# Attention and mixture-of-experts layer on one core: 32 expert pairs in two alternating scatter chains, four tables loaded together at the end, last block reordered

## The chip, the cores and the metric

The kernel runs on one core of one Trainium2 chip. The metric is the device time of one execution in microseconds (us); lower is better. The times shown are medians of several executions, and a profile is one further execution.

## The reference

The input x has 4 sequences of 1024 tokens with 256 values each. Two sublayers follow one another, each with a layer norm ahead and a layer norm behind it, and a residual sum.

```python
x = x + _layernorm(attn(_layernorm(x)))   # 16 heads, 4 key/value heads, head size 128, causal, rope
x = x + _layernorm(ffn(_layernorm(x)))    # 64 experts, 6 for each token, plus a shared expert
# ffn, per token t:   y[t] = sum over its experts e of w[t,e] * down_e(silu(x @ gate_e) * (x @ up_e))
#                     out[t] = y[t] + down_s(silu(x @ gate_s) * (x @ up_s))
# routing: top 4 of 8 groups, then the 6 best of 64 experts; at most 48 tokens for an expert
```

## The kernel before

Three blocks of instructions follow one another, and no engine enters the next block before all engines have left the last. The function attention fills the span up to about 1781 us. It is not changed. The function last_quad follows (to about 1847 us), and then the function experts (to the end).

**last_quad** finishes what is left of the last 512 tokens: the norms of y and x1, the logits, the choice of experts, and the lists of tokens of every expert (VectorE's largest, rounds of MAX8 and MATCH_REPLACE8). Beside that the shared expert runs over eight parts of 512 tokens: gate_up and down on TensorE, gate_tanh and shared_out on ScalarE, shared(n) on VectorE, which consists of two instructions (lines 1535 and 1540). shared_out(n) sends its part to the first of four tables in HBM, named sums, by a DMA that ScalarE issues (line 1444). ScalarE's last instructions in this block wait for all these DMAs (y_out, line 1487). Near the end GpSimd stores the routing weights (line 1495), waits for all seven of its stores and for seven counts of index_done, and issues six gathers of token rows (line 1514, LEAD = 6). Its memset of the gather buffer (line 1498) stands ahead of the first inverse root, for whose result VectorE waits before it applies x1 (line 1555). SyncE loads the weights of 40 experts into w_early.

**experts** works through 32 pairs of experts. For pair j TensorE transposes the gathered rows (line 1863), multiplies by gate and up (1875), transposes the hidden values (1883) and multiplies by down (1890). ScalarE and VectorE copy and scale the halves of the result (1829, 1768) into a ring of four y buffers. GpSimd then adds the 128 rows to the tables in HBM by an indirect DMA with an add (line 1729). The rows of one expert never meet twice, but rows of different pairs may, so a scatter waits until the one before it in its chain has landed. There are two chains with two tables each:

```python
def in_second(j):
    return j % 2 == 1 and j < 2 * TURNS      # TURNS = 14
```

So the second chain holds 14 pairs, the last one pair 27, and pairs 28 to 31 all go to the first chain, one after another. A buffer of y is filled again when the scatter four pairs back has landed. Ahead of each scatter GpSimd issues the gather of the pair LEAD ahead, once VectorE and TensorE have let go of the buffer (ring of 8).

SyncE loads the last 24 experts (line 1694), then x1 (1696), and, when the second chain has ended, its two tables m2 and m3 into the space of used weights (1702), unit by unit. A unit is 4 tiles of 128 tokens; there are 8. VectorE adds m3 to m2 (joined, line 1779) in between the last steps of the pair loop, two units in each of the last four steps. When the first chain has ended, SyncE loads m0 and m1, each unit after its join (1709).

The last stage works unit by unit: GpSimd adds m2 to m0 (1742), TensorE adds m0 and m1 in PSUM by an identity matrix (1912), VectorE takes the statistics (1793, 1796) and the reciprocal (1801), ScalarE the root (1845) and the scaling (1853), GpSimd the shift (1737, 1738), VectorE adds the residual (1785), SyncE stores (1713). The small tiles of this stage are rings of two, and residual(u-1) stands between the statistics and the reciprocal of unit u.

## Time and profile before

| what | value |
|---|---|
| median of 3 executions | 2049.85 us (2048.86 to 2051.9) |
| the profiled execution's own time | 2050.17 us |
| its span, first to last instruction | 2048.4 us |
| mean granted TensorE clock | 0.956 of full speed |
| busy share of the span: TensorE matmul, VectorE, ScalarE, GpSimd | 93%, 65%, 56%, 63% |
| last_quad | 1781 to 1847 us |
| pair loop, first matmul to last scatter landed | 1847 to 1990 us |
| last stage | 1990 to 2048 us |

The span is what the rows below are measured in; 1.77 us of the profiled execution's time lie around it. The busy shares are averages over very different stages: TensorE's 93% come from attention, and in the last 200 us it is often idle. Times in the rows are microseconds from the start of the span.

### The profile page before, as it was taken

The numbers are of one execution on the slowest core, as the hardware profiler recorded it, in microseconds if no ns is written. First come the engines' busy times: TensorE is split into PE (matmuls) and PEld (weight loads), VectorE is DVE, ScalarE is ACT, GpSimd is POOL, SyncE is SP. The second block draws the span as 40 slices with busy tenths as digits, with TensorE's granted clock in tenths as the row PEclk, the third lists the DMA queues.
The fourth block names the chain that finished last, engine by engine and source line by source line (L and its number), as shares of the span: only waits on it lengthen the run. The fifth ranks groups of instructions, "written<-read, shape, count | busy, mean of one in ns | idle before, by whom it ended". The sixth has DMA issues, their size and how long they took to land. (4 is left out here: it accounts for less than half of the span.)

```text
span 2048.4 us, 34361 instructions
## 1 busy us (share of the span) xinstructions
PE 1895.5 (93%) x11846; PEld 1566.2 (76%) x11846; DVE 1330.8 (65%) x3149; ACT 1154.0 (56%) x2632; POOL 1284.4 (63%) x1061
## 2 busy tenths in 40 slices
PE   5999999999999999999999999999999999787926
PEld 4888888888888888888888888888888888543412
DVE  5566666667767677777667667676676778762324
ACT  3556666666656665566565665666655655333413
POOL 5758576666666765758485766676666755214733
PEclk8999999999999999999999999999999999995658
DMA  5005000001110100000100100001101000298476
GB/s 178 16 27 164 29 21 6 22 6 31 48 52 6 42 1 22 11 27 32 58 21 6 42 6 27 6 21 57 32 6 42 1 17 17 105 357 284 67 220 210
DMA packets 77292, 120.22 MB, mean 59 GB/s; under 512 B 9639, under 2 KB 57717, under 8 KB 75873
## 3 DMA queue, kind: packets, MB, share of 16 engines
q1 hardware_dynamic: 65264, 92.61, 13.6%
q0 software_dynamic: 7248, 12.72, 2.6%
q10 hardware_dynamic: 4608, 12.68, 1.9%
q8 instruction: 98, 1.61, 0.3%
q14 instruction: 74, 0.60, 0.1%
HBM read 90.34 MB, written 38.53 MB: 63 GB/s over the span
## 5 line engine op out<-in xcount | busy, mean ns | idle before, releaser
L561 PE MATMUL s_ps<-kT,q 128*128 128x512 f32 (+3 forms) x2304 | 584.3, 371 | 13.9 <-POOL q L1136 7.9
L824 DVE TENSOR_TENSOR pT<-t_ps,pT 128x512 fp32r<-128x512 f32 (+3 forms) x768 | 401.0, 550 | 191.0 <-ACT pT L969 189.8
L811 DVE TENSOR_REDUCE neg_max<-s_ps 128x1 f32<-128x640 f32 (+7 forms) x512 | 384.6, 751 | 110.8 <-PE s_ps L561 103.9
L561 PEld LDWEIGHTS s_ps<-kT,q 128*128 128x128 f32 x2304 | 408.3, 192 | 61.6 <-ACT probs L958 11.6
L586 PE MATMUL av_ps<-pT,v 128*128 128x512 f32 x1728 | 442.2, 400 | 2.7 <-DVE pT L824 2.7
L1121 POOL TENSOR_TENSOR k_roped<-raw,sinT 64x512 f32<-64x512 f32 x316 | 406.7, 1287 | 24.3
L969 ACT ACTIVATE pT<-t_ps 128x512 fp32r<-128x512 f32 (+3 forms) x768 | 348.7, 490 | 129.8 <-PE t_ps L571 125.0
L958 ACT ACTIVATE probs<-s_ps,neg_max 128x640 f32<-128x640 f32 (+7 forms) x512 | 381.9, 746 | 63.3 <-DVE neg_max L811 61.0
L586 PEld LDWEIGHTS av_ps<-pT,v 128*128 128x128 f32 x1728 | 311.8, 189 | 67.1 <-DVE pT L824 7.8
L571 PE MATMUL t_ps<-k_ident,probs 128*128 128x128 f32 x2304 | 340.1, 274 | 11.6 <-DVE pT L824 7.9
L1118 POOL TENSOR_TENSOR k_roped<-raw,cosT 128x512 f32<-128x512 f32 x158 | 204.4, 1294 | 220.1 <-ACT raw L930 201.3
L571 PEld LDWEIGHTS t_ps<-k_ident,probs 128*128 128x128 f32 x2304 | 263.2, 140 | 37.4 <-ACT probs L958 12.8
L598 PE MATMUL misc_ps<-w_o,avT 128*128 128x256 f32 x1536 | 237.9, 291 | 15.5 <-DVE y L856 8.1
L598 PEld LDWEIGHTS misc_ps<-w_o,avT 128*128 128x128 f32 x1536 | 204.9, 189 | 33.5 <-ACT raw L930 12.9
L856 DVE SCALAR_TENSOR_TENSOR y<-misc_ps,inv_sum,y 128x256 f32<-128x256 f32 x448 | 214.9, 480 | 14.1 <-PE misc_ps L598 6.1
L1123 POOL TENSOR_TENSOR raw<-k_roped 128x512 f32<-128x512 f32 x158 | 202.8, 1283 | 12.4
L518 PE MATMUL misc_ps<-xT,w_q 128*128 128x256 f32 x1524 | 204.2, 283 | 1.7 <-DVE y L856 1.7
L518 PEld LDWEIGHTS misc_ps<-xT,w_q 128*128 128x128 f32 x1524 | 194.6, 190 | 3.7 <-DVE y L856 2.3
L829 DVE TENSOR_TENSOR avT<-av_ps,avT 128x512 fp32r<-128x512 f32 x128 | 88.6, 692 | 136.5 <-ACT avT L976 136.3
L976 ACT ACTIVATE avT<-av_ps 128x512 fp32r<-128x512 f32 x128 | 76.3, 596 | 162.2 <-PE av_ps L586 159.5
L939 ACT ACTIVATE q<-raw 128x512 fp32r<-128x512 f32 x128 | 80.6, 630 | 150.7 <-POOL raw L1123 150.7
L1136 POOL TENSOR_TENSOR q<-raw,q 128x512 fp32r<-128x512 f32 x128 | 163.1, 1288 | 1.8 <-ACT q L939 1.8
(245 smaller groups left out, 1877.4 us busy)
## 6 DMA issues: line engine op xcount, KB each, us to landing
w_early<-in_expert_w SPq DMA_DIRECT2D x5, 2560.0 KB, 26.6
w_early<-sums SPq DMA_DIRECT2D x24, 512.0 KB, 8.8
k_staged<-in_wpack SPq DMA_DIRECT2D x47, 256.0 KB, 2.9
sums<-sums ACTq DMA_DIRECT2D x2, 4144.0 KB, 22.9
k_staged<-in_wpack SPq DMA_DIRECT2D x16, 512.0 KB, 3.7
e_w_late<-in_expert_w SPq DMA_DIRECT2D x3, 2560.0 KB
k_xw<-in_x SPq DMA_DIRECT2D x4, 1024.0 KB, 5.8
k_xb<-in_x SPq DMA_DIRECT2D x4, 1024.0 KB, 5.9
```

The costliest lines, as they stand in the source:

```text
L518: last = pe.matmul(bank("q", macro, half)[:, h * 256:(h + 1) * 256], w_q[:, s, half, c, h * HD:(h + 1) * HD], pair(xT[:, b % 2, a, c], m), ...
L561: last = pe.matmul(out, q[:, macro % 2, a, h, int(big)], kT[:, g % 2, s, lo:hi], start=(n == 0), stop=(n == 2))
L571: last = pe.transpose(t_ps[n % 2][:, j * P:(j + 1) * P], probs[:, r % 3, (first + j) * P:(first + j + 1) * P], ident[:])
L586: last = pe.matmul(av_ps[:], v[:, g % 2, a, j], pT[:, s, part_slot(p) + j], start=(j == 0 and n == 0), stop=(j == blocks - 1 and n == 2))
L598: last = pe.matmul(misc_ps[:, h * HID:(h + 1) * HID], avT[:, a, 2 * half + h], w_o[:, s, 2 * half + h], start=(n == 0), stop=(n == 2))
L811: dve.reduce_max(neg_max[:, r % 16:r % 16 + 1], s_ps[:, r % 2, 0:(row_tile(r) + 1) * P], AX.X, negate=True).then_inc(max_ready, 1)
L824: dve.tensor_tensor(lo, t_ps[n % 2][:, 0:count * P].rearrange("p (j n) -> p j n", n=P), hi.bitcast(F32), ALU.subtract).then_inc(t_lo, 1)
L856: last = dve.scalar_tensor_tensor(target[:, t], src, inv, y[:, t], ALU.mult, ALU.add)
L958: act.activation(probs[:, r % 3, 0:width], s_ps[:, r % 2, 0:width], ACT.Exp, bias=neg_max[:, r % 16:r % 16 + 1], accum_out=row_sum[:, r % ...
L969: act.activation(pT[:, 0, slot + first:slot + first + count, r % 4], t_ps[n % 2][:, 0:count * P].rearrange("p (j n) -> p j n", n=P), ACT.C ...
L1118: pool.tensor_tensor(shape(cosed), shape(raw[:, n % 2]), table(cosT, 0, P), ALU.mult).then_inc(cos_done, 1)
L1121: pool.tensor_tensor(shape(rope[64 - lo:128 - lo]), shape(raw[lo:hi, n % 2]), table(sinT, lo, hi), ALU.mult).then_inc(sin_done, 1)
```

## The change

In last_quad: TensorE's down(0) goes ahead of transpose_x2, ScalarE's gate_tanh(1) ahead of x1_apply. VectorE's shared(0) is split, its first half goes ahead of the x1 step, and shared(1) goes from the third round of largest to the place after shared_up(0). GpSimd's memset goes behind the row stores. The four instructions that make the routing weights go from the end of VectorE's work to the place ahead of the second set of rounds. LEAD becomes 8, so eight gathers are issued. ScalarE's wait for y_out leaves the block; SyncE takes it as its first instruction in experts, and GpSimd ahead of its first scatter.

In experts: TURNS becomes 16, so the chains alternate to the end with 16 pairs each. The early load and the joins inside the pair loop are gone. After the pair loop SyncE loads all four tables unit by unit; VectorE adds m3 to m1 while GpSimd adds m2 to m0, TensorE sums the two, and the last unit is summed by VectorE alone. LAG = 2 makes the small tiles rings of three, and the residual of a unit comes after the join of the unit three behind it.

```diff
-TURNS = 14
+TURNS = 16
+LAG = 2
-    RING, LEAD = 8, 6
+    RING, LEAD = 8, 8
...
             gate_up(1)
+            down(0)
             transpose_x2()
-            down(0)
...
             gate_tanh(0)
+            gate_tanh(1)
             x1_apply()
-            gate_tanh(1)
...
-            for i in range(2):
-                act.wait_ge(y_out[i], 32 * B)
...
-            link(pool.memset(index.gathered[:], 0.0))
...
+            link(pool.memset(index.gathered[:], 0.0))
             pool.wait_ge(weight_done, 1)
             store_weights(LAST)
             pool.wait_ge(stored, 7 * 16)
-            pool.wait_ge(index_done, 7)
+            pool.wait_ge(index_done, 5)
...
             stats(xw, kept.y_mv)
             dve.memset(last_rows[:], 0.0)
+            shared_gate(0)
             dve.wait_ge(rstd_done, 1)
...
-            shared(0)
+            shared_up(0)
+            shared(1)
...
-                if i == 2:
-                    shared(1)
...
             shared(3)
+            (product, sum, reciprocal and scale of the routing weights)
             dve.wait_ge(key_in, 1)
...
-            (the same four instructions)
...
         def _(sp):
+            for i in range(2):
+                sp.wait_ge(y_out[i], 32 * B)
...
-            sp.wait_ge(y_ready, last_pair(2))
-            sp.wait_ge(added[1], 16 * TURNS)
-            for u in range(UNITS):
-                for dst, table in ((m2, 2 * TABLE), (m3, 3 * TABLE)):
-                    sp.dma_start(unit(dst, u), ...).then_inc(loaded[u], 16)
             sp.wait_ge(y_ready, PAIRS)
             sp.wait_ge(added[0], 16 * (PAIRS - TURNS))
             for u in range(UNITS):
-                sp.wait_ge(joined, u + 1)
-                for dst, table in ((m0, 0), (m1, TABLE)):
+                for n, dst in enumerate((m0, m1, m2, m3)):
+                    if u == 0 and n == 2:
+                        sp.wait_ge(added[1], 16 * TURNS)
                     sp.dma_start(unit(dst, u), ...).then_inc(loaded[u], 16)
...
+                if j == 0:
+                    for i in range(2):
+                        pool.wait_ge(y_out[i], 32 * B)
...
-                for u in range(max(first, 0), first + 2):
-                    dve.wait_ge(loaded[u], 32)
-                    dve.tensor_tensor(unit(m2, u), unit(m2, u), unit(m3, u), ALU.add).then_inc(joined, 1)
...
+            def join(u):
+                dve.wait_ge(loaded[u], 64)
+                if u < UNITS - 1:
+                    dve.tensor_tensor(unit(m1, u), unit(m1, u), unit(m3, u), ALU.add).then_inc(joined, 1)
+                else:
+                    dve.tensor_tensor(unit(m1, u), unit(m1, u), unit(m3, u), ALU.add)
+                    link(dve.tensor_tensor(unit(m0, u), unit(m0, u), unit(m2, u), ALU.add))
+                    link(dve.tensor_tensor(unit(m0, u), unit(m0, u), unit(m1, u), ALU.add))
...
+            for u in range(UNITS):
+                join(u)
+                if u:
+                    stats_of(u - 1)
+                if u > LAG:
+                    residual(u - LAG - 1)
+            stats_of(UNITS - 1)
+            for u in range(UNITS - LAG - 1, UNITS):
+                residual(u)
...
             for u in range(UNITS):
                 root_of(u)
+                if u:
+                    scale_of(u - 1)
+            scale_of(UNITS - 1)
...
-            for u in range(UNITS):
+            for u in range(UNITS - 1):
                 pe.wait_ge(padded, u + 1)
+                pe.wait_ge(joined, u + 1)
```

## Rows read from the trace of the kernel before

**Rows 1.** Timeline of SyncE's queue, 1840 to 1995: start, issue time, line, tensors, count.

```profile
1847.22 5.93 SPq L1694 DMA_DIRECT2D e_w_late<-in_expert_w  x3
...
1957.01 20.55 SPq L1702 DMA_DIRECT2D w_early<-sums  x16
1990.16 0.36 SPq L1709 DMA_DIRECT2D e_w_late<-sums  x1
```

**Rows 2.** Timeline of VectorE, first join: start, duration; in brackets idle time before it.

```profile
1963.34 1.23 DVE L1779 TENSOR_TENSOR w_early<-w_early 128x1024 f32<-128x1024 f32 x1 [8.13 <-DMA w_early<-sums]
```

**Rows 3.** Chain of work that ended last: start, length, what.

```profile
1856.33 8.20 DMA sums<-k_xb,i_to_row
...
1881.51 10.02 DMA i_gathered<-rows,i_from_row
...
1953.30 3.64 DMA sums<-k_xb,i_to_row
...
1969.43 8.11 DMA sums<-k_xb,i_to_row
...
2024.83 3.71 PE e_gu_ps L1912 x8
```

**Rows 4.** Timeline of GpSimd in last_quad.

```profile
1783.09 2.25 POOL L1498 MEMSET i_gathered<- 128x2560 f32 x1
...
1829.64 1.41 POOL L1495 DMA_DIRECT2D rows<-k_row_w  x2 [33.52 <-DVE k_row_w L1609]
1836.29 1.11 POOL L1514 DMA_INDIRECT i_gathered<-rows,i_from_row  x1 [5.24 <-DMA rows<-k_row_w]
```

**Rows 5.** Timeline of VectorE in last_quad.

```profile
1787.33 1.67 DVE L1555 SCALAR_TENSOR_TENSOR k_xb<-k_xw,k_y_rstd,k_xb 128x256 f32<-128x256 f32 x4 [4.15 <-POOL k_shift L248]
...
1793.04 0.73 DVE L1563 TENSOR_SCALAR k_xw<-k_xb,k_x_mv,k_x_rstd 128x256 f32<-128x256 f32 x2 [0.68 <-POOL k_x_shift L246]
...
1797.49 0.68 DVE L1535 SCALAR_TENSOR_TENSOR r_a<-r_th,r_gate 96x512 f32<-96x512 f32 x1
...
1827.79 0.42 DVE L1606 TENSOR_TENSOR k_spare<-k_score,k_picked 128x256 f32<-128x256 f32 x1
...
1829.25 0.18 DVE L1612 TENSOR_SCALAR i_from_row<-r_c 128x32 int32<-128x32 f32 x1
```

**Rows 6.** Timeline of ScalarE in last_quad: first tanh, last output issue.

```profile
1784.73 0.59 ACT L1434 ACTIVATE r_th<-r_gate 96x512 f32<-96x512 f32 x1 [5.10 <-PE r_gate L1356]
...
1840.51 0.98 ACTq L1444 DMA_DIRECT2D sums<-r_y  x2
```

**Rows 7.** Timeline of GpSimd, the scatters of pairs 8 and 28.

```profile
1891.19 1.60 POOL L1729 DMA_INDIRECT sums<-k_xb,i_to_row  x1 [1.89 <-DMA sums<-k_xb,i_to_row]
...
1956.28 1.55 POOL L1729 DMA_INDIRECT sums<-k_xb,i_to_row  x1 [1.43 <-issue]
```

**Rows 8.** Busy time by stretch: PE, PEld, DVE, ACT, POOL, clock, DMA share, GB/s.

```profile
1820.00:1830.00 10.00, 6.90 (x28) 4.02 (x27) 7.43 (x33) 2.28 (x4) 0.36 (x1) 0.94 1.04 403
...
1900.00:1910.00 10.00, 10.00 (x45) 4.14 (x43) 2.63 (x9) 3.76 (x12) 7.97 (x7) 0.50 0.40 66
...
2000.00:2005.00 5.00, 5.00 (x10) 2.21 (x9) 0.85 (x3) 0.00 (x0) 1.00 (x1) 0.72 1.10 348
```

**Rows 9.** Timeline of VectorE in the last stage.

```profile
2020.45 1.38 DVE L1785 TENSOR_TENSOR e_w_late<-e_w_late,w_early 128x1024 f32<-128x1024 f32 x1 [0.31 <-ACT e_w_late L1853]
...
2038.25 1.43 DVE L1793 BATCH_NORM_STATS2 e_stats<-e_y_ps 128x6 f32<-128x256 f32 x4 [0.99 <-PE e_y_ps L1912]
...
2043.84 1.23 DVE L1785 TENSOR_TENSOR e_w_late<-e_w_late,w_early 128x1024 f32<-128x1024 f32 x1 [2.55 <-ACT e_w_late L1853]
```

**Rows 10.** Timeline of GpSimd in the last stage, one unit's add.

```profile
2018.41 2.34 POOL L1742 TENSOR_TENSOR e_w_late<-e_w_late,w_early 128x1024 f32<-128x1024 f32 x1
```

**Rows 11.** Timeline of ScalarE, root and scaling of the last unit.

```profile
2040.12 0.30 ACT L1845 ACTIVATE e_root<-e_mv,e_eps 128x4 f32<-128x4 f32 x1 [0.35 <-DVE e_mv L1796]
2041.87 1.93 ACT L1853 ACTIVATE e_w_late<-e_y_ps,e_shift,e_rstd 128x256 f32<-128x256 f32 x4 [1.45 <-POOL e_shift L1738]
```

More of the change, by code:

```diff
@@ L1284, in __init__, with last_quad @@
         self.from_row, self.to_row = sb("from_row", [P, EXPERTS // 2], I32), sb("to_row", [P, EXPERTS // 2], I32)
-def last_quad(nc, consts, kept, index, rows, x1_rows, x2t_rows, y_rows, w_early, w_in, shared_in, gathered_in):
+def last_quad(nc, consts, kept, index, rows, x1_rows, x2t_rows, y_rows, w_early, w_in, shared_in, gathered_in, y_out):
     with ExitStack() as ctx:
@@ L1319, in last_quad @@
         gate_ready, up_ready, tanh_done, a_done, h_done = (sem(n) for n in ("gate_ready", "up_ready", "tanh_done", "a_done", "h_done"))
-        down_ready, y_read, y_out = sem("down_ready"), sem("y_read"), [sem(f"y_out{i}") for i in range(2)]
+        down_ready, y_read = sem("down_ready"), sem("y_read")
         block = ctx.enter_context(nc.Block())
@@ L1540, in shared @@
                 dve.scalar_tensor_tensor(h[:, n % 2], a[:, n % 2], 0.5, up_ps[n % 2][0:FF], ALU.mult, ALU.mult).then_inc(h_done, 1)
+            def shared(n):
+                shared_gate(n)
+                shared_up(n)
             def largest(at, left, i):
@@ L1619, in _, with experts @@
             shared(7)
-def experts(nc, consts, kept, rows, index, w_early, w_in, gathered_in, sums, x1_rows, out):
+def experts(nc, consts, kept, rows, index, w_early, w_in, gathered_in, sums, x1_rows, y_out, out):
     with ExitStack() as ctx:
@@ L1696, in _ @@
             sp.dma_start(x1.rearrange("p (b t) n -> p b t n", b=B), x1_rows.rearrange("b p t n -> p b t n")).then_inc(x1_in, 16)
-            sp.wait_ge(y_ready, last_pair(2))
-            sp.wait_ge(added[1], 16 * TURNS)
-            for u in range(UNITS):
-                first = u * UNIT * P
-                for dst, table in ((m2, 2 * TABLE), (m3, 3 * TABLE)):
-                    sp.dma_start(unit(dst, u), tiles(sums[table + first:table + first + UNIT * P])).then_inc(loaded[u], 16)
             sp.wait_ge(y_ready, PAIRS)
@@ L1706, in _ @@
                 first = u * UNIT * P
-                sp.wait_ge(joined, u + 1)
-                for dst, table in ((m0, 0), (m1, TABLE)):
-                    sp.dma_start(unit(dst, u), tiles(sums[table + first:table + first + UNIT * P])).then_inc(loaded[u], 16)
+                for n, dst in enumerate((m0, m1, m2, m3)):
+                    if u == 0 and n == 2:
+                        sp.wait_ge(added[1], 16 * TURNS)
+                    at = n * TABLE + first
+                    sp.dma_start(unit(dst, u), tiles(sums[at:at + UNIT * P])).then_inc(loaded[u], 16)
             for u in range(UNITS):
@@ L1842, in root_of, with scale_of @@
                 act.wait_ge(mv_ready, u + 1)
-                if u >= 2:
-                    act.wait_ge(rstd_ready, u - 1)
-                act.activation(root[:, u % 2], mv[:, u % 2, :, 1], ACT.Sqrt, bias=eps[:]).then_inc(root_done, 1)
+                if u > LAG:
+                    act.wait_ge(rstd_ready, u - LAG)
+                act.activation(ring(root, u), ring(mv, u)[:, :, 1], ACT.Sqrt, bias=eps[:]).then_inc(root_done, 1)
+            def scale_of(u):
+                act.wait_ge(shift_ready, u + 1)
+                for t in range(UNIT):
+                    last = act.activation(m0[:, u * UNIT + t], summed_tile(u, t), ACT.Identity, bias=ring(shift, u)[:, t:t + 1], scale=ring(rstd, u)[:, t:t + 1])
+                last.then_inc(normed, 1)
             act.wait_ge(act_done, 1)
@@ L1850, in _ @@
                 root_of(u)
-                act.wait_ge(shift_ready, u + 1)
-                for t in range(UNIT):
-                    last = act.activation(m0[:, u * UNIT + t], summed_tile(u, t), ACT.Identity, bias=shift[:, u % 2, t:t + 1], scale=rstd[:, u % 2, t:t + 1])
-                last.then_inc(normed, 1)
+                if u:
+                    scale_of(u - 1)
+            scale_of(UNITS - 1)
         @block.tensor
@@ L1902, in _ @@
                     down(s - 3)
-            for u in range(UNITS):
+            for u in range(UNITS - 1):
                 pe.wait_ge(padded, u + 1)
+                pe.wait_ge(joined, u + 1)
                 if u >= 4:
@@ L1929, in build @@
         gathered_in = [ctx.enter_context(nc.semaphore(f"gathered_in{i}")) for i in range(index.RING)]
-        last_quad(nc, args, kept, index, rows, x1_rows, x2t_rows, sums[0:TABLE], w_early, w_in, shared_in, gathered_in)
-        experts(nc, args, kept, rows, index, w_early, w_in, gathered_in, sums, x1_rows, out)
+        y_out = [ctx.enter_context(nc.semaphore(f"y_out{i}")) for i in range(2)]
+        last_quad(nc, args, kept, index, rows, x1_rows, x2t_rows, sums[0:TABLE], w_early, w_in, shared_in, gathered_in, y_out)
+        experts(nc, args, kept, rows, index, w_early, w_in, gathered_in, sums, x1_rows, y_out, out)
 def lay_out(inputs):
```

70 lines of the change are left out of this document (41 added, 29 removed).

## The prediction

> **What bounds the kernel now.** I read the chain of work that ended last first, because the busy shares say little about the last 270 us, where the whole change lies. From 1847 us on the chain is made of three things in turn: scatters and gathers whose landing somebody awaits, TensorE's matmuls, and then the summing stage [rows 3]. The timeline of SyncE's queue gives the three marks to keep: the last load of weights at 1847.22, the early load of two tables from 1957.01, and the first load of the other two at 1990.16 [rows 1]. From this last mark to the end of the span are 2048.4 - 1990.2 = 58.2 us.
>
> The reader should look at what happens between 1957 and 1990. The early load lies beside the last pairs. VectorE takes its queue in order, and its first join stands ahead of its work for pairs 30 and 31. It sat 8.13 us for the first unit's tables [rows 2] and then for the next. So the scatter of pair 29, due about 1960 (pair 28's at 1956.28 and a landing [rows 7]), went out at 1969.43, and under the load it took 8.11 us to land, where the one at 1953.30 took 3.64 [rows 3]. Three such scatters in one chain end at 1990. In the last stage the load of 8 units is not what holds: at 348 GB/s [rows 8] a unit of two tables, 1.05 MB, takes 3.01 us, and the whole stage takes 58.2.
>
> **The change part by part.**
>
> *Head, last_quad.* (a) Without the memset, 2.25 us [rows 4], the first inverse root ends that much sooner. VectorE applied x1 at 1787.33 [rows 5]. But the new shared_gate(0) stands ahead of it and needs the first tanh, which ends at 1784.73 + 0.59 = 1785.32 [rows 6], then takes 0.68 [rows 5]. So x1 starts at 1786.0: 1.3 us sooner. (b) shared(1), two instructions of 0.68, leaves the rounds of largest. It goes where VectorE sat 0.68 us for the second inverse root [rows 5], together with the half of shared(0) that moved forward: these two hide it. Gain 1.4, in all 2.7. Who is late now: nobody, since TensorE's down(0) ahead of the transposes falls into its own idle time before x2 is ready, and the logits come sooner, well ahead of VectorE. (c) The four instructions of the weights, 1829.25 - 1827.79 = 1.46 us [rows 5], now lie ahead of the rounds: the lists end at 1827.8 - 2.7 + 1.5 = 1826.6. TensorE turns them, which the weights used to hide, some 0.5 us, and the index is there about 1827.7. (d) GpSimd issued the first gather at 1836.29 because the weights' stores of 1829.64 had to land first [rows 4]. Those stores now go out well over 10 us sooner, because six rounds of largest and six smaller ones lie behind them, so the gathers start about 1828. Eight of them at 1.1 + 0.3 take 11 us and are issued by 1839.3. (e) The block ended with the landing of the shared outputs, at 1847.2 [rows 1], although ScalarE had issued the last at 1840.51 + 0.98 = 1841.5 [rows 6]. The wait is moved; the last issue is 1.2 sooner with the rest, 1840.3; I allow 1.0 for the meeting of the engines. experts starts at 1841.3, which is 5.9 us sooner. The moved waits: behind SyncE's stand the last weights and x1, which nobody needs for 40 us or more; behind GpSimd's stands the first scatter, whose rows are ready about when the outputs land, near 1846. If that cover were gone, the 5.9 would shrink to about 1. Bounds of the head: 1 to 7.
>
> *First pairs.* SyncE's bulk loads (12 MB: w_late and x1) start at the landing of y_out, so hardly sooner than before, and now run together. While they run a scatter takes 8.2 us [rows 3] and each chain holds one at a time, so pairs 0, 2, 4, 6, 8 follow one another at about 9 us, later less. With pair 0 at 1850.4 (1856.33 - 5.9) and loads that end about 1877, I get 1859.5, 1868.5, 1876.5 and pair 8 at 1883; before it was at 1891.19 [rows 7]. The 2.3 us beyond the head's 5.9 come from LEAD = 8: before, a gather of 10.02 us held TensorE [rows 3], and now it is issued two pairs sooner. The nearest bounds are 3 us (the bulk loads eat the head start) and 14.
>
> *Rest of the pair loop.* Before, pairs 8 to 28 took 1956.28 - 1891.19 = 65.1 us, 3.25 each [rows 7]: GpSimd's gather and scatter, or TensorE at half clock, 45 matmuls of 15 a pair in 10 us, 3.3 a pair [rows 8]. The new kernel has both, so I keep 65.1. Then three more, alternating, each after the landing of the one two back: (3.64 + 0.7) / 2 = 2.2 us each, 6.5. So pair 31 goes out at 1883 + 65.1 + 6.5 = 1954.6 and pair 30's landing starts the load at 1954.6 - 2.2 + 3.64 + 0.5 = 1956.5. Before, that mark was 1990.2. Of the 33.7 us between them 8.2 come from pair 8, and 25.5 from the last pairs: four scatters in one chain without stall or load would have ended about 1973 (1956.3 + 4 x 4.3), so 17 are the collision that is gone and 8 the alternation. Bounds: 1951, if TensorE has its full clock and GpSimd's eight pairs without a gather go at 2.2; 1967, if the half clock holds 3.5 us a pair to the end.
>
> *Load.* The price of the change: all 16 portions of 1.05 MB (two transfers each) now stand behind the pair loop. The first landed 1963.34 - 1957.01 = 6.3 us after its issue [rows 1, 2], the other 15 follow at 3.01: 51.5 us, and 1.1 us for the second portion, which waits for pair 31, in all 52.6. The rate is from a stretch without other work [rows 8]. The last unit is there at 1956.5 + 52.6 = 2009.1. Other work hides below it: a unit takes 6.0 us to load, GpSimd needs 2.34 [rows 10] and two small ones, TensorE 3.71 [rows 3], VectorE 1.23 for the join, 1.87 + 0.3 for statistics and root, 1.23 for the residual [rows 9, 11], so none is the bound. The stores come after the loads in SyncE's queue; six of 1.5 us fit below the tail.
>
> *Tail after the last unit.* VectorE sums it alone, 3 x 1.23 = 3.7. Then the statistics of unit 6 through its reciprocal, 2.4 with 0.2 for the reciprocal; residual 4, 1.23; statistics of unit 7 to the root's start, 2040.12 - 2038.25 = 1.9; root 0.3; ScalarE's scaling of units 6 and 7, because root 7 stands ahead of scale 6: 2 x 1.93; residual 1.23; then 2048.4 - 2045.07 = 3.3 for the store [rows 9, 11]. Sum 17.9.
>
> Before the tail stands one wait that the trace shows only at its edge. VectorE's residual at 2020.45 started while GpSimd's add of 2018.41 to 2020.75 ran, and took 1.38 instead of 1.23 [rows 9, 10]: an overlap of 0.3 cost 0.15. In the new stage GpSimd's add and VectorE's join start on the same semaphore in every unit. If one waits out the other, the join ends 2.34 + 1.23 after the landing, and VectorE's round of 4.8 us ends 7.2 after it. That is 1.2 more than the 6.0 of a unit, but it does not add up: the next join then asks 1.2 later and waits 1.2 less. The last unit has no such add, so the cost is 1.2 once. I take it, as if the wait were full, and keep 0 and 2.3 as its bounds; with the half that the row shows it would be 0.6. The Trainium skill ("SBUF — State Buffer", Who interferes with whom) says that VectorE with two SBUF inputs and GpSimd reading SBUF exclude each other for a whole instruction. By that rule the sum comes out as below, and by the half wait of the row 0.6 us sooner; at its edge the trace agrees in direction.
>
> **Sum.** 1956.5 + 52.6 + 1.2 + 17.9 = 2028.2 us of span; with 1.77 around it 2030.0, against 2050.17 of the profiled execution, 20.2 us less. The median of the runs is 0.3 below that execution, so 2029.7; I say 2030.
>
> **The rivals.**
>
> *TensorE keeps the half clock.* It ran at 0.50 through 1900 to 1910 though busy all the time [rows 8], so being busy doesn't bring it back at once. At that level, 1.2 GHz, the pair loop takes up to 3.5 us a pair and starts the load at 1967; in the sums a unit is 7.4 us (2 x 3.71) instead of 6.0, so unit 6 lags. For it: GpSimd's waits are gone, so TensorE is nearer to being the bound. Against: the clock was 0.72 and rising after 5 us of summing [rows 8]. With the pair loop alone at half clock the time is 2040.
>
> *All smooth.* Pair loop at full clock, bulk loads over sooner, load from 1951 or before: 2024.
>
> *The loads go faster than 348 GB/s.* The tables' own stretch does not, but from 1820 to 1830, with expert weights in larger rows, 403 GB/s were moved [rows 8]. At that pace 16.8 MB take 6.6 us less: 2023. The Trainium skill ("DMA: Bandwidth & Descriptors", Measured) has 425 GB/s for 16 MB in one piece; by that figure it would be 2021, an estimate from that page. The row of the same tensors speaks against it.
>
> *Slower: the load of four tables collapses.* The transfers now alternate among four regions of HBM. If a transfer took over 4.4 us instead of 3.01 (240 GB/s), 15 of them would eat the whole gain: that is the point from which it decides. At 220 GB/s it is 2056. For it: half of these bytes lay beside other work before and are now in the open, so every loss of rate counts twice. Against: two regions in turn already run at the full 348 [rows 8], and two more are the same kind of read.
>
> *It does not do what it says.* The head's gain and LEAD = 8 are taken back by bulk loads, and VectorE or the ring of y holds pairs 28 to 31 as before: 2050. The code leaves no wait of that kind.
>
> **How the numbers follow.** Forecast 0.60 (2030, its own range 2026 to 2035). Half clock 0.16 (2040), all smooth 0.11 (2024), faster loads 0.04 (2023), collapse 0.06 (2056), no gain 0.03 (2050). The range 2021 to 2041 leaves out the last two and the edges of the others, and it holds the bounds of the head (3 us less gained) and of the pair loop (5.5 us sooner to 10.5 later). Faster by over 0.2%, which is 4.1 us and about what a measurement of this kernel can tell from no change: 0.60 + 0.16 + 0.11 + 0.04 = 0.91; within it 0.03; slower 0.06.
>
> **What would show it.** First matmul of the block experts about 1841 and first gather about 1828 (before 1836.3). Scatter of pair 8 about 1883. No idle time of VectorE over 3 us between 1940 and 1955, and scatters of pairs 29 to 31 about 2.2 us apart. SyncE's first table load about 1956.5, 32 of them, units 6.0 us apart at 348 GB/s, the last landed about 2009. GpSimd's add and VectorE's join one after the other. 19 us from the last landing to the end. The prediction is wrong if the pair loop's bulk loads hold more than two scatters at 8 us each, if TensorE falls behind the loads, or if the rate is below 300 GB/s.

## The result, and the profile after

The median of the runs of the new kernel is 2030.77 us (2028.52 to 2033.01), that of the kernel before, run beside it, 2050.82: a ratio of 0.9906 with the interval 0.9893 to 0.9918. It is faster by 20.1 us, and the forecast was 2030. The profiled execution of after took 2028.52 us with a span of 2026.6, so 1.9 us lie around it. Attention ended later in it, and last_quad starts 1.07 us later than in the trace of before (1782.21 against 1781.14). All marks below are as the trace has them; where the shift matters I say so.

SyncE's queue (start and length in us, then line, operation and tiles) has the three marks that [rows 1] had:

```profile
1844.96 5.39 SPq L1711 DMA_DIRECT2D e_w_late<-in_expert_w  x3
...
1956.89 0.93 SPq L1722 DMA_DIRECT2D e_w_late<-sums  x2
1960.11 0.91 SPq L1722 DMA_DIRECT2D w_early<-sums  x2
```

The first table load goes out at 1956.89, as early as the old early load did, but now all 32 scatters lie before it. The two loads of 1960.11 are those of m2 and m3, which had to wait for pair 31. From there to the last load SyncE waits for nothing but its own queue.

GpSimd's timeline shows how the pair loop gets there (in brackets the idle time before, and what ended it):

```profile
1829.83 1.12 POOL L1512 DMA_INDIRECT i_gathered<-rows,i_from_row  x1 [14.67 <-DVE i_to_row L1622]
...
1854.31 1.63 POOL L1745 DMA_INDIRECT sums<-k_xb,i_to_row  x1 [0.30 <-issue]
...
1880.93 1.60 POOL L1745 DMA_INDIRECT sums<-k_xb,i_to_row  x1 [1.83 <-DMA sums<-k_xb,i_to_row]
...
1888.82 1.60 POOL L1745 DMA_INDIRECT sums<-k_xb,i_to_row  x1 [0.30 <-issue]
...
1937.54 1.60 POOL L1745 DMA_INDIRECT sums<-k_xb,i_to_row  x1 [0.30 <-issue]
...
1942.14 1.55 POOL L1745 DMA_INDIRECT sums<-k_xb,i_to_row  x1 [1.12 <-DMA sums<-k_xb,i_to_row]
...
1955.63 1.55 POOL L1745 DMA_INDIRECT sums<-k_xb,i_to_row  x1 [1.05 <-DMA sums<-k_xb,i_to_row]
1965.90 3.37 POOL L1759 TENSOR_TENSOR e_w_late<-e_w_late,w_early 128x1024 f32<-128x1024 f32 x1 [8.72 <-DMA w_early<-sums]
```

These are, in order, the first gather, then the scatters of pair 0, 6, 8, 23, 25 and 31, and the first add. Three stages can be told apart by what stands in the brackets. Up to pair 7 a landing releases half of the scatters (pairs 2, 5, 6 and 7), VectorE or TensorE most of the others. From pair 8 to pair 23 it is the issue itself: (1937.54 - 1888.82) / 15 = 3.25 us a pair, and GpSimd never waits. The last eight have no gather ahead of them, and go (1955.63 - 1937.54) / 8 = 2.26 us apart, and every odd pair goes out at the landing of the one two back, with an even pair close behind it. Pair 29 follows pair 28 after 2.46 us, where 13 us separated them in [rows 3, 7].

The chain of work that ended last, for the scatters in it and for the last load (start, length, what):

```profile
1857.61 7.47 DMA sums<-k_xb,i_to_row
...
1866.30 9.02 DMA sums<-k_xb,i_to_row
...
1946.59 3.65 DMA sums<-k_xb,i_to_row
...
1955.63 4.46 DMA sums<-k_xb,i_to_row
...
2000.36 8.67 DMA w_early<-sums
```

Beside the bulk loads a scatter takes 7.5 to 9.0 us to land, without them 3.65, as in [rows 3]. The last scatter, with two table loads beside it, takes 4.46. The last stage, on VectorE:

```profile
1978.37 3.01 DVE L1804 TENSOR_TENSOR e_w_late<-e_w_late,w_early 128x1024 f32<-128x1024 f32 x1
...
2009.05 1.23 DVE L1806 TENSOR_TENSOR w_early<-w_early 128x1024 f32<-128x1024 f32 x1 [1.16 <-DMA w_early<-sums]
...
2022.08 1.23 DVE L1799 TENSOR_TENSOR e_w_late<-e_w_late,w_early 128x1024 f32<-128x1024 f32 x1 [0.73 <-ACT e_w_late L1882]
```

VectorE waits 1.16 us for the last unit, which is there at 2009.05. So the loads bound this stage until their end, and what follows is a tail of 2026.6 - 2009.05 = 17.55 us.

### The profile page after: what moved, and what is told of

Its sections match the earlier page's. It is cut to its first block and busy times, and to the rows that moved or that the text cites. A ratio compares the mean times of both kernels' runs of the same rounds, so it can differ in the third digit from the quotient of the medians.

```text
span 2026.6 us, 34344 instructions
## 1 busy us (share of the span) xinstructions
PE 1883.1 (93%) x11838; PEld 1560.8 (77%) x11838; DVE 1337.4 (66%) x3149; ACT 1149.0 (57%) x2632; POOL 1292.7 (64%) x1060
## 5 line engine op out<-in xcount | busy, mean ns | idle before, releaser
L1123 POOL TENSOR_TENSOR raw<-k_roped 128x512 f32<-128x512 f32 x158 | 202.9, 1284 | 12.4
```

## The experiments

Twelve kernels. All times are medians; the ratio is to the kernel before, run beside each of them (its medians were 2051.21 for the three b kernels and a_turns14, 2051.24 for a_lag1 to a_x1_paced, 2049.88 for the rest).

| kernel | us | ratio and interval |
|---|---|---|
| before | 2050.82 | |
| after | 2030.77 | 0.9906 (0.9893 to 0.9918) |
| b_join_after | 2045.13 | 0.9968 (0.9955 to 0.9980) |
| b_load_after | 2057.26 | 1.0031 (1.0020 to 1.0042) |
| b_head | 2042.06 | 0.9953 (0.9936 to 0.9969) |
| a_turns14 | 2037.93 | 0.9932 (0.9915 to 0.9948) |
| a_lag1 | 2035.54 | 0.9921 (0.9905 to 0.9938) |
| a_half_load | 2016.81 | 0.9834 (0.9818 to 0.9851) |
| a_no_join | 2026.95 | 0.9885 (0.9869 to 0.9902) |
| a_x1_paced | 2023.60 | 0.9867 (0.9851 to 0.9883) |
| a_all_paced | 2027.76 | 0.9886 (0.9870 to 0.9903) |
| a_tail | 2028.36 | 0.9897 (0.9880 to 0.9913) |
| a_best | 2024.29 | 0.9876 (0.9859 to 0.9892) |
| a_best_all | 2024.51 | 0.9876 (0.9859 to 0.9892) |

Two things blur small differences. Executions of after alone spread over 4.5 us. And last_quad, ahead of which no kernel was changed, starts anywhere from 1779.69 (a_tail) to 1783.73 (a_all_paced) in the traces. So where a difference is under 5 us I look for its place in the traces, from a mark behind that start.

**b_join_after**: the kernel before, with VectorE's joins moved behind its pair loop. It leaves the early load where it was and takes only the stall.

```diff
-                first = 2 * (s - (PAIRS + 3 - UNITS // 2))
-                for u in range(max(first, 0), first + 2):
-                    dve.wait_ge(loaded[u], 32)
-                    dve.tensor_tensor(unit(m2, u), unit(m2, u), unit(m3, u), ALU.add).then_inc(joined, 1)
...   (behind the loop over pairs)
+            for u in range(UNITS):
+                dve.wait_ge(loaded[u], 32)
+                dve.tensor_tensor(unit(m2, u), unit(m2, u), unit(m3, u), ALU.add).then_inc(joined, 1)
```

> The kernel before, with VectorE's eight joins of the two early tables moved behind the pair loop; the early load itself stays where it is. It takes away VectorE's stall and leaves the collision of the early load with the last scatters. Theory A (stall and collision overlap, and either alone holds the last four scatters back): scatters of pairs 29 to 31 go out without VectorE's wait but take 7 to 8 us each under the load, the first load of the other tables moves from 1990 to about 1985, and the time falls by 3 to 6 us, to about 2045. Rival B (the stall alone is the cost): that mark goes to about 1974 and the time falls by 14 to 17 us, to about 2034.

2045.13 us, 6 us less than before. GpSimd's timeline, from the scatter of pair 29 on:

```profile
1960.45 1.55 POOL L1729 DMA_INDIRECT sums<-k_xb,i_to_row  x1 [3.07 <-DMA sums<-k_xb,i_to_row]
1968.59 2.56 POOL L1729 DMA_INDIRECT sums<-k_xb,i_to_row  x1 [6.59 <-DMA sums<-k_xb,i_to_row]
...
```

Pair 29 goes out at 1960.45, where I had it "due about 1960", and not at 1969.43. But pairs 30 and 31 then wait 6 us each for a landing, because the early load lies beside them. The load of m0 starts 6 us sooner than the 1990.16 of before:

```profile
1984.18 0.36 SPq L1709 DMA_DIRECT2D e_w_late<-sums  x1
```

The stall alone is worth 6 us, 5.5 of them from pair 28's scatter on, and the rival, that it was the whole cost, falls.

**b_load_after**: the same, and the early load goes behind the last scatter too (SyncE waits for all of y and both added semaphores before it).

```diff
-            sp.wait_ge(y_ready, last_pair(2))
+            sp.wait_ge(y_ready, PAIRS)
             sp.wait_ge(added[1], 16 * TURNS)
+            sp.wait_ge(added[0], 16 * (PAIRS - TURNS))
             for u in range(UNITS):
                 first = u * UNIT * P
                 for dst, table in ((m2, 2 * TABLE), (m3, 3 * TABLE)):
...
```

> The kernel before, with the load of the two early tables and their joins both moved behind the pair loop, chains still 14 and 18. Neither stall nor collision is left; 16 portions of 1.05 MB stand in the open. Theory A: the last four scatters follow one another at 4.3 us, the loads start at about 1973, take 50 us, and with a tail of 12 to 15 us the span ends at 2036 to 2040; time about 2039, 10 to 12 us less than before. Rival C (the added load in the open costs all that the collision cost): 2050.

2057.26 us: slower than before by 6, where I expected it faster. The pair loop did what was expected of it; the last stage did not. SyncE's first load and GpSimd's first add and the wait before it:

```profile
1972.55 18.98 SPq L1703 DMA_DIRECT2D w_early<-sums  x16
```

```profile
1968.70 1.55 POOL L1728 DMA_INDIRECT sums<-k_xb,i_to_row  x1 [3.07 <-DMA sums<-k_xb,i_to_row]
2002.04 2.33 POOL L1741 TENSOR_TENSOR e_w_late<-e_w_late,w_early 128x1024 f32<-128x1024 f32 x1 [31.78 <-DMA w_early<-sums]
```

The scatters of pairs 28 to 31 are 4.5 us apart and the last goes out at 1968.70, so stall and load together had cost the pair loop 1986.0 - 1968.7 = 17.3 us. But eight units of m2 and m3 now stand ahead of the first of m0 and m1, and the first add waits for them until 2002.04. From there to the end are 52.7 us, as in before (2048.4 - 1995.65 = 52.75). At 3.01 us for a unit's two tables the loads of m0 and m1 would need half of that. So the old last stage was not bound by its loads. Its chain, the same in both kernels, shows what held it; here a stretch of b_load_after:

```profile
2028.75 2.31 POOL e_w_late L1741
2031.10 3.71 PE e_gu_ps L1911 x8
2034.84 1.44 DVE e_stats L1792 x4
...
2037.70 0.18 DVE e_rstd L1800
...
2038.23 0.20 POOL e_shift L1737
2038.43 2.30 POOL e_w_late L1741
```

GpSimd's queue has the shift of one unit ahead of the add of the next but one, and that shift needs the add, TensorE's sum, VectorE's statistics, the root and the reciprocal of its own unit: a ring of 9.68 us for two units (2038.43 - 2028.75). In after, LAG = 2 lets GpSimd's add run ahead of that ring, and the loads bring all four tables of a unit together, so that the first add can start early. Loading late alone gives up the cover that the pairs gave, 24 us of loads, for the 17 us.

**b_head**: the kernel before with the whole of the head's edits, LEAD = 8 and the wait for y_out moved, but with TURNS = 14, the early load and the joins in the pair loop as before.

```diff
 # before, with last_quad of after; to_row written for TURNS = 14
-    RING, LEAD = 8, 6
+    RING, LEAD = 8, 8
...
         def _(sp):
+            for i in range(2):
+                sp.wait_ge(y_out[i], 32 * B)
...
+                if j == 0:
+                    for i in range(2):
+                        pool.wait_ge(y_out[i], 32 * B)
                 pool.wait_ge(y_odd, j + 1)
```

> The kernel before with the head of the change alone: the reordered last_quad, the moved wait for the outputs, and eight gathers ahead. Chains, early load, joins and last stage are those of before. The prediction put 8.2 us on this part up to the scatter of pair 8; the trace of the changed kernel shows that scatter only 3.4 us sooner once the later start of the block is taken off. Theory A: 3 to 7 us less than before, about 2045, the part above 3.4 from the last eight pairs that have no gather between them. Rival B: the prediction's 8 us or more, 2042.

2042.06 us, 9 us less, which is more than I expected: the number is that of the rival. Its reason is not. Pair 8 goes out at 1887.49 (1891.19 before), 3.7 us sooner, and the early load at 1949.39 instead of 1957.01, 7.6 sooner; so half of the gain comes behind pair 8, as theory A had it. No run takes LEAD = 8 apart from the reordered block. The collision is still there, at the same pair:

```profile
1947.50 1.55 POOL L1738 DMA_INDIRECT sums<-k_xb,i_to_row  x1 [0.71 <-issue]
1962.47 2.57 POOL L1738 DMA_INDIRECT sums<-k_xb,i_to_row  x1 [13.42 <-DVE k_xb L1777]
```

The scatter of 1962.47 is that of pair 29; it waited 13.42 us for VectorE, which sat at a join.

**a_turns14**: after, with the second chain cut back to 14 scatters, so that the last four pairs again share one chain.

```diff
-TURNS = 16
+TURNS = 14
...
-            first, second = (slice(k, EXPERTS // 2, 2) for k in range(2))
+            second, first = slice(1, 2 * TURNS, 2), (slice(0, 2 * TURNS, 2), slice(2 * TURNS, EXPERTS // 2))
```

> The changed kernel with 14 pairs in the second chain again, so pairs 28 to 31 are one chain. Theory A: these four go out 4.4 us apart instead of 2.3, the load starts 5 to 8 us later, and the time is 5 to 8 us above the changed kernel's, about 2037. Rival B (the last pairs are held by TensorE or the ring of y buffers, not by the chain): no difference, 2030.

2037.93 us, 7.2 more than after. The last two scatters of its timeline:

```profile
...
1958.25 1.55 POOL L1745 DMA_INDIRECT sums<-k_xb,i_to_row  x1 [3.11 <-DMA sums<-k_xb,i_to_row]
1962.84 1.55 POOL L1745 DMA_INDIRECT sums<-k_xb,i_to_row  x1 [3.04 <-DMA sums<-k_xb,i_to_row]
```

They are 4.6 us apart instead of 2.26, and the loads start 9.8 us after those of after:

```profile
1966.66 0.92 SPq L1722 DMA_DIRECT2D e_w_late<-sums  x2
```

The prediction had 8 for the alternation.

**a_lag1**: after, with the rings of the last stage one shorter.

```diff
-LAG = 2
+LAG = 1
```

> The changed kernel with LAG = 1: small tiles in rings of two and every step of the last stage one unit closer, as in the kernel before. Joining after the load, unit by unit, stays. Theory A (the load of 6.0 us a unit is the bound, so the deeper rings only give slack): within 2 us of the changed kernel, 2030. Rival B (with rings of two the waits between engines exceed 6.0 us a unit, as the stage of before took 5 to 6 us a unit with no load to wait for): 1 us or more a unit, 2038 or more.

2035.54 us, 4.8 more than after: between my two theories, and neither was right. VectorE in its later units:

```profile
1998.81 2.29 DVE L1799 TENSOR_TENSOR e_w_late<-e_w_late,w_early 128x1024 f32<-128x1024 f32 x1 [1.64 <-ACT e_w_late L1882]
...
2006.16 2.29 DVE L1799 TENSOR_TENSOR e_w_late<-e_w_late,w_early 128x1024 f32<-128x1024 f32 x1 [1.64 <-ACT e_w_late L1882]
```

With LAG = 1 the residual belongs to the unit whose scaling has only just begun, so VectorE waits 1.64 us for ScalarE in every unit, and the residual then falls beside GpSimd's add and takes 2.29 instead of 1.2. The unit grows to 2006.16 - 1998.81 = 7.35 us, more than the 6.02 of its loads. In this trace 78.3 us pass from the first table load to the end, against 69.7 in after.

**a_half_load**: after without the loads of m2 and m3.

```diff
-                for n, dst in enumerate((m0, m1, m2, m3)):
-                    if u == 0 and n == 2:
-                        sp.wait_ge(added[1], 16 * TURNS)
+                if u == 0:
+                    sp.wait_ge(added[1], 16 * TURNS)
+                for n, dst in enumerate((m0, m1)):
...   (the adds then wait for 32 instead of 64)
```

> The changed kernel without the loads of tables m2 and m3; the adds still run, on what lies in their place. The summed result leaves out two tables. Theory A (the load is the bound, and without half of it the engines are: VectorE's round of 4.8 us a unit, plus what it waits for GpSimd): the stage falls from 6.0 to about 4.8 us a unit, 8 to 12 us less than the changed kernel, about 2020. Rival B (nothing but the load matters): 24 us less, 2006. Rival C (the load was hidden by the engines): 0 to 3 us less.

2016.81 us, 14 less than after, a little more than the 8 to 12 of theory A. If loads were all of it, it would have been 24. From the third unit on VectorE never waits for data, and units settle at 4.6 us: that is the floor of the stage's arithmetic, 1.4 us a unit below the loads. Two of VectorE's joins, one unit apart:

```profile
1983.28 1.21 DVE L1804 TENSOR_TENSOR e_w_late<-e_w_late,w_early 128x1024 f32<-128x1024 f32 x1
...
1987.85 1.21 DVE L1804 TENSOR_TENSOR e_w_late<-e_w_late,w_early 128x1024 f32<-128x1024 f32 x1
```

**a_no_join**: after without VectorE's add of m3 to m1 in units 0 to 6.

```diff
-                    dve.tensor_tensor(unit(m1, u), unit(m1, u), unit(m3, u), ALU.add).then_inc(joined, 1)
+                    dve.sem_inc(joined, 1)
```

> The changed kernel without VectorE's joins of units 0 to 6, so table m3 is left out of those sums. It takes away the one add of VectorE that meets GpSimd's add. Theory A (the two exclude each other while both read SBUF): GpSimd's adds take 2.34 us each instead of 3.38, and the time stays within 2 us of 2030, since the load is the bound. Rival B (GpSimd's adds are slower for another reason, such as the loads running beside them): they stay at 3.4.

2026.95 us, 3.8 less than after, with an interval for the ratio that overlaps that of after by a little. GpSimd's add in the second unit, to be held against the 3.37 above:

```profile
1970.48 2.34 POOL L1759 TENSOR_TENSOR e_w_late<-e_w_late,w_early 128x1024 f32<-128x1024 f32 x1 [3.68 <-DMA w_early<-sums]
```

So the two engines do hold each other up, and it is VectorE's join that makes the add long. The profiled execution, 2026.68 us, is 1.8 below that of after, and its first table load went out 1.85 us sooner (1955.04), ahead of anything that was left out. From that load to the end it takes 69.8 us, after 69.7. So nothing was gained there, which is what I expected of it. The 3.8 us lie between medians of four runs each, and I can place no more of them.

**a_x1_paced**: after, with x1 loaded in eight parts, one every second pair from the ninth on, instead of whole once TensorE has done seven.

```diff
-            sp.wait_ge(y_ready, last_pair(0))
-            sp.dma_start(x1.rearrange("p (b t) n -> p b t n", b=B), x1_rows.rearrange("b p t n -> p b t n")).then_inc(x1_in, 16)
+            for b in range(B):
+                for half in range(2):
+                    sp.wait_ge(y_ready, X1_FROM + X1_STEP * (2 * b + half))
+                    sp.dma_start(x1[:, b * NT + 4 * half:b * NT + 4 * half + 4], x1_rows[b][:, 4 * half:4 * half + 4]).then_inc(x1_in, 16)
```

> The changed kernel with the load of x1, 4.2 MB, in eight parts, one at every second pair from pair 9 on, instead of one load at pair 7. Theory A (bulk loads hold the scatters, each 7 to 9 us instead of 3.7 while they run, which is the step that the prediction sized wrong): the scatters of pairs 5 to 8 come closer, pair 8 goes out 3 to 5 us sooner and the time falls by 3 to 5 us, to about 2026. Rival B (what holds the first pairs is GpSimd's own issue of 3.25 us a pair): no difference.

2023.60 us, 7.2 less than after and more than the 3 to 5 that I expected: the fastest kernel of all. A stretch by windows in both, first after and then a_x1_paced. The columns are the window, its length, busy us of PE, PEld, DVE, ACT and POOL, the granted clock, the share of the DMA engines and GB/s:

```profile
1863.00:1873.00 10.00, 9.33 (x41) 4.21 (x41) 2.79 (x9) 2.39 (x11) 6.87 (x5) 0.50 1.06 379
```

```profile
1863.00:1873.00 10.00, 6.53 (x37) 2.88 (x35) 2.99 (x9) 3.33 (x12) 6.82 (x6) 0.81 0.64 184
```

In after x1's 4 MB keep the DMA engines full until 1880. In a_x1_paced the load is over with w_late, and the pair loop comes to its 3.25 us a pair from pair 5 on. Its scatter of pair 8:

```profile
1882.88 1.60 POOL L1748 DMA_INDIRECT sums<-k_xb,i_to_row  x1 [0.30 <-issue]
```

That is 29.6 us after pair 0, where after takes 34.5. Nearly all of these 4.9 us lie at pairs 5 to 7, whose scatters in after waited 1.70 to 2.08 us each for a landing and here go out 3.25 apart. The granted clock differs too in this stretch, 0.50 against 0.81, but what released these scatters in after was a landing and not TensorE's work. The parts of x1 then go out from 1873 to 1920, beside the scatters of pairs 5 to 19, and cost them nothing, since these are bound by GpSimd's issue. The two traces are 5.0 us apart in span, so the 4.9 are all that they show; the rest of the 7.2 I can't place.

One thing in the last stage of this kernel is new. VectorE's join of unit 6 and its first add of the last unit:

```profile
1997.33 3.37 DVE L1807 TENSOR_TENSOR e_w_late<-e_w_late,w_early 128x1024 f32<-128x1024 f32 x1
2004.02 1.22 DVE L1809 TENSOR_TENSOR w_early<-w_early 128x1024 f32<-128x1024 f32 x1
```

Two joins in a row, of units 5 and 6, came second to GpSimd's add and took 3.37 us. VectorE has no idle time left before the last unit, and the chain that ended last runs through both joins. From the first load to the end it takes 70.4 us, after 69.7.

**a_all_paced**: the same, and w_late in twelve parts, the first two at once and each other after a further pair, with x1 from pair 12 on.

```diff
+            for k in range((EXPERTS - EARLY) // 2):
+                e = EARLY + 2 * k
+                if k >= 2:
+                    sp.wait_ge(y_ready, k - 1)
+                sp.dma_start(w_late[:, 2 * k:2 * k + 2], consts["expert_w"][e:e + 2].rearrange("e p n -> p e n")).then_inc(w_in[e // (2 * LOADS)], 16)
```

> The changed kernel with x1 in eight parts (from pair 12 on, every second pair), and the last 24 experts' weights in twelve loads of two experts each, one a pair, instead of three loads of eight at once. Theory A: the first eight pairs then run nearly at 3.25 us like the later ones, pair 8 goes out at about 1881 instead of 1888.8, and with the x1 part the time falls to about 2019. Rival B (paced loads of weights only spread the same collision over more pairs, and the gathers wait instead): no less than the kernel with x1 alone, 2023.6.

2027.76 us, where I expected 2019. From pair 0 to pair 8 it takes 29.9 us, as a_x1_paced does (29.6): spreading w_late as well carries its loads on to 1879, beside pairs that ran undisturbed, and gains nothing, as the rival said. That the median lies 4.2 above a_x1_paced says little: in its trace last_quad started 3.05 us later, ahead of all that was changed.

**a_tail**: after, with residual 4 ahead of the last unit's adds, and the first of these adds started on m0 and m1 before m2 and m3 are there.

```diff
+                    residual(u - LAG - 1)
+                    for k, (dst, src) in enumerate(((m0, m1), (m2, m3))):
+                        dve.wait_ge(*((loaded[u], 32), (x1_in, 48))[k])
+                        link(dve.tensor_tensor(unit(dst, u), unit(dst, u), unit(src, u), ALU.add))
```

> The changed kernel with the last unit's sum in three steps, each as its tables land (m0 + m1 after the first two transfers), and residual 4 ahead of it. Theory A (the tail of 17.5 us behind the last landing is a chain of VectorE's queue): two adds and one residual leave it, 3.6 us less, 2027. Rival B (the tail is ScalarE's or the store's): under 1 us.

2028.36 us, with an interval that overlaps that of after. From the first table load (1954.18) to the end its trace takes 72.4 us, against 69.7. It shows why the edit brought nothing:

```profile
2008.88 1.22 DVE L1801 TENSOR_TENSOR e_w_late<-e_w_late,w_early 128x1024 f32<-128x1024 f32 x1 [0.53 <-ACT e_w_late L1886]
2010.02 1.22 DVE L1811 TENSOR_TENSOR e_w_late<-e_w_late,w_early 128x1024 f32<-128x1024 f32 x1
```

Residual 4 had to wait for ScalarE's scaling until 2008.88, and the first add, free to start before the last load, stood behind it until 2010.02. The wait was only exchanged for another. In this trace TensorE's sum of unit 5, which ScalarE's queue needs before that scaling, also ran at a lower clock (0.68 from 2000 to 2005, where after had 1.00). That is not the whole cause: in a_best and a_best_all the clock was 1.00 there, and residual 4 waited the same 0.53 us.

**a_best** and **a_best_all** put the edit of a_tail on a_x1_paced and on a_all_paced.

> x1 in eight parts from pair 9 on, and the last unit's sum in three steps, together. The two lie in different stages, so both gains should add: 7.2 and 3.6 us less than the changed kernel, about 2020. If the tail step gains nothing, 2023.6.

> x1 in eight parts, the last weights in twelve paced loads, and the last unit's sum in three steps. If pacing the weights gains what is expected of it, about 2016, the fastest of all; if it gains nothing, as the kernel with x1 in parts and the new tail.

2024.29 and 2024.51 us, no better than a_x1_paced alone: the tail's edit is worth nothing there either (72.3 us from first load to end in both, against 70.4), and with it the two ways of pacing are 0.2 us apart. The version to keep is a_x1_paced, 27.6 us below the 2051.24 of the kernel before, run beside it.

## Why the prediction was right

Against the steps of the prediction, with its own numbers:

| term | predicted | measured | difference |
|---|---|---|---|
| first matmul of experts | 1841.3 | 1844.12 | +2.8 |
| pair 0's scatter after it | 9.1 | 10.2 | +1.1 |
| pair 0 to pair 8 | 32.6 | 34.5 | +1.9 |
| pair 8 to pair 31 | 71.6 | 66.8 | -4.8 |
| pair 31 to the first table load | 1.9 | 1.3 | -0.6 |
| load, all 16 portions | 52.6 | 52.2 | -0.4 |
| port wait | 1.2 | 0 | -1.2 |
| tail | 17.9 | 17.55 | -0.35 |

The sum of the differences is -1.6, that is 2026.6 instead of 2028.2 of span.

**Head.** 1.07 of the 2.8 us are the later start of last_quad in this execution. The steps (a) and (b) hold: x1 starts at 1787.22, expected 1786.0 and the shift, and the index is there at 1828.22, against 1827.7 and the shift. The first gather no longer waits for the weights' stores but for the index, 1829.83. What I mis-sized is the end of the block: ScalarE's last issue ended 0.9 later than I had, the shift taken off (it sat idle for 0.87 us ahead of its last copy instead of 0.21), and the engines took 1.85 us from ScalarE's last issue to the first matmul, for which I allowed 1.0. b_head, with these edits and LEAD = 8 alone, is 9 us faster than before.

**First pairs.** The bulk loads start only 2.3 us sooner, as argued, and scatters took 7.5 and 9.0 us beside them. I had the loads end about 1877; they ended at 1880, and pair 8 came 5.8 us after my mark with the head's part in it. That is the very edge of its bounds, 3 to 14 us sooner than before: it was 2.4 as the trace has it, outside, and 3.4 without the shift, inside. a_x1_paced shows that the term was real and avoidable: without x1 in this stretch it is 4.9 us shorter. One sign of being wrong that the prediction named did come: the bulk loads held more than two scatters at about 8 us (7.47 and 9.02 above, and pairs 2, 5, 6 and 7 waited for landings). It was badly chosen, for the sum itself had three in one chain at 8 to 9 us each.

**Rest of the loop.** Mis-sized by as much in the other direction. I kept 65.1 us for the pairs up to 28 and read them as one pace of 3.25. They were three. In before, pairs 13 to 20 went out (1932.38 - 1907.62) / 7 = 3.54 us apart:

```profile
1907.62 1.60 POOL L1729 DMA_INDIRECT sums<-k_xb,i_to_row  x1 [0.50 <-issue]
...
1932.38 1.60 POOL L1729 DMA_INDIRECT sums<-k_xb,i_to_row  x1 [0.60 <-issue]
```

That is TensorE's pace at half clock, not GpSimd's. After has 3.25 up to pair 23, 2.2 us less for pairs 8 to 23. And GpSimd has no gather to issue for the last eight, where before had six such: 3.1 us less for pairs 23 to 28. I had this as the lower bound of the range ("GpSimd's eight pairs without a gather go at 2.2") and not as the value. 15 x 3.25 + 8 x 2.26 = 66.8, and the last three pairs took 0.5 more than my 6.5. The bound had TensorE's full clock as a condition. In after it was met, from 1910 on, but a_all_paced shows that it isn't needed: TensorE was at half clock there through 1930 to 1940 and its matmuls had half-clock length until 1946, yet the scatters from pair 23 to 31 went out (1953.21 - 1934.56) / 8 = 2.33 us apart. Its lead was enough.

```profile
1930.00:1940.00 10.00, 10.00 (x44) 4.31 (x45) 3.00 (x9) 4.05 (x13) 7.55 (x6) 0.50 0.62 116
```

The two errors, +5.8 and -5.4 with the step to the load, cancelled: that the load's start at 1956.89 is right against 1956.5 is luck in its parts, though not in its mechanism. Without that luck the time would have been up to 6 us off either way, still inside the range.

**Where the time went.** The prediction split the last pairs into 17 us of collision and 8 of alternation. b_load_after has 17.3 for the first, of which b_join_after has 6 for VectorE's stall alone, and a_turns14 has 9.8 for the second in its trace, 7.2 in its median. What it did not see is why the old last stage took its time: it read from [rows 8] only that the load didn't hold it. b_load_after shows the ring through GpSimd's shift. The saving of 20 us is a sum of three that hang together. Going back from b_load_after's span of 2054.7: with the head's edits and LEAD = 8 the loads start 1972.55 - 1966.66 = 5.9 us sooner (against a_turns14), with two full chains 1966.66 - 1956.89 = 9.8 more, and from the first load to the end after needs 69.7 us where b_load_after needs 82.2, which is 12.4 (a_lag1 puts 8.6 of a trace's span on LAG; what the order of the loads and VectorE's joins are worth by themselves no run shows). Together 28.1, as between the two spans; less the 6.3 that b_load_after's span lies above that of before, it is the 21.8 between 2048.4 and 2026.6.

**Load and tail.** Portions of 6.02 us a unit at 348 GB/s over the four regions; the rivals of faster loads and of a collapse both fall. The window of after in the middle of the load:

```profile
1990.00:2000.00 10.00, 4.78 (x11) 1.63 (x9) 9.51 (x20) 3.04 (x8) 6.75 (x4) 1.00 1.10 348
```

a_half_load confirms that loads, and not arithmetic, set the pace in after, but by less than the prediction's "none is the bound" suggests: 4.6 against 6.02. VectorE is busy 9.51 of 10 us here. With the port wait on top its margin is thin, as the last stage of a_x1_paced shows.

**Port wait.** The whole wait is there, as the rows above show: GpSimd's add took 3.37 instead of the 2.34 of [rows 10] where VectorE's join got in first (3.37 or 3.38 in five of seven), and where GpSimd was first the join took 3.01 and 3.37 instead of 1.23. The Trainium skill ("SBUF — State Buffer", Who interferes with whom) has the two exclude each other for a whole instruction, and these rows agree. The term in the sum was still wrong: nothing of it reached the end, because VectorE had caught up and sat idle for 1.16 us before the last landing. In after the right value was the lower bound, 0. That is no general result: in a_x1_paced, where two joins in a row came second, the wait lies on the chain that ended last.

**Half clock.** The rival was there and did not decide. In the trace of after, by windows, the granted clock was at 1.2 GHz (0.50) through 1870 to 1910 and at 2.4 GHz after it:

```profile
1900.00:1910.00 10.00, 10.00 (x45) 4.31 (x44) 2.95 (x9) 3.66 (x11) 8.08 (x7) 0.50 0.41 68
1910.00:1920.00 10.00, 8.64 (x64) 4.34 (x62) 3.75 (x11) 4.66 (x16) 7.96 (x7) 0.97 0.40 66
```

At half clock its matmuls of a pair filled 3.54 us in the chain, GpSimd needs 3.25. Yet the scatters kept their 3.25 from pair 8 to pair 23, so TensorE was far enough ahead until the full clock came back. In before, where the half clock lasted until 1930, it was not, and pairs 13 to 20 went at 3.54. So the rival was nearer than the time shows. At 0.29 us a pair over 15 pairs it would have cost about 4 us, an estimate from these two paces, and not the ten that it was given.

## What to carry to other kernels

A wait in an in-order queue costs what stands behind it: look for the engine that sits at a load which nobody needs yet, and for what its next instructions hold up, here three scatters of one chain (6 us for the stall, 17 with the load beside them). Moving the load out of the way is not enough by itself (it cost 6 us here); it pays once all tables of a unit are loaded together, so that each unit starts as it lands, and the rings are deep enough that no engine's next unit stands behind the last one's tail. Bulk loads that nobody needs for long belong in parts beside work that an engine's issue bounds, and not beside transfers whose landing somebody awaits: x1 in eight parts was worth 4.9 us in the trace and 7.2 between the medians.

## What the runs showed of the hardware

- A scatter that adds 128 rows of 1 KB into HBM lands 3.64 to 3.79 us after its issue, also when two chains alternate (4.46 us with two table loads beside it); beside bulk loads at 375 to 392 GB/s it takes 7.5 to 9.0 us. Beside x1 in parts, at 109 to 164 GB/s in all, GpSimd's 3.25 us a pair is not disturbed.
- GpSimd's issue bounds the pairs: 1.04 + 0.30 us for a gather and 1.60 + 0.30 for a scatter, 3.25 us together.
- TensorE stayed at 1.2 GHz through windows in which it was busy all the time (10.00 of 10.00 from 1900 to 1910) and came back to 2.4 GHz in the next, with the same matmuls to do. In before it stayed there until 1930, in a_x1_paced it fell twice. I can't say what released it.
- Two full-size adds, one on GpSimd and one on VectorE, share nothing of their time when they start together: 3.37 us is 2.34 and nearly all of 1.23.
